# Three edits to a four-layer block: how expert weights are split, how combination weights are made, and in which order side steps run

## The chip, the cores and the metric

One core of a Trainium2 chip runs the whole program. The metric is the device time of one execution in microseconds; three runs of the kernel before gave a median of 966.74 us. A profile was taken of one more execution.

## What is computed

Four rows of 1024 tokens by 128 features pass through four residual layers: a linear attention of its own kind, a mixture of experts (MoE), a windowed softmax attention, and the same MoE again. Only the MoE is touched by the arithmetic of the change:

```python
logits = x @ gate_w.T
probs = jax.nn.softmax(logits.astype(jnp.float32), axis=-1)
top_w, top_idx = jax.lax.top_k(probs, TOP_K)          # 8 of 32 experts
top_w = top_w / jnp.sum(top_w, axis=-1, keepdims=True)
...
gu = x @ guw.T
g, u = jnp.split(gu, 2, axis=-1)
y = u * jax.nn.silu(g) @ dw.T                         # weighted by comb, summed over experts
```

## The kernel before

**Stages.** A row is cut into two halves of 512 tokens (four tiles of 128). Every half passes twice through the MoE, which makes 16 MoE stages of 16 chunks; a chunk is two experts. For a chunk TensorE forms gate and up (`gate_up`, lines 1519 to 1521: six products), ScalarE applies silu (L1056), VectorE multiplies by up (L1304), GpSimd multiplies by the combination weights spread over the partitions (L872), and TensorE adds the down product to one bank (L1542). Work tiles form a ring of 6. The windowed attention is a stretch of its own in each row: eight tiles, each with scores, maxima (VectorE), exponentials (ScalarE, L1081), a normalisation (GpSimd, L880), transpositions and their copies (VectorE, L1346) and the mix. The order is the list `SCHEDULE`: period 0 has the stages "first" and "third" and then "attn" of row 0; later periods interleave two rows.

**Side steps.** Everything else (norms, q/k/v, linear attention, router, combination weights, projections) is cut into named steps. The table `PLAN` says behind which chunk of a stage, or behind which of three hooks of an attention tile (slot 0 to 26), a step stands; every engine runs its own part of a step at that place of its own queue, in order. `own`, `ahead` and `back` choose the row: this period's, the next, the one before. The list `AHEAD` is the order of all that comes before the first chunk; this stretch is called the opening here. Steps that go through PSUM share one bank, `side`, in the order of the plan.

Steps that the prediction speaks of: `x_stats` (VectorE norm statistics, waits for the load of the row's half), `attend` (GpSimd key-value terms), `kvsum`, `wterm`, `wred` (VectorE, linear attention), `qkv`/`qkv_next` (TensorE and ScalarE), `h_...` (head norms), `moe_turn`, `z_hi`, `z_lo` (the MoE's input, transposed and split), `route`, `r_sum`, `top` (router logits and their eight largest), `weigh` (ScalarE: exponentials), `comb` (VectorE: keep the chosen, sum, reciprocal), `cnorm` (ScalarE), `weighT` (transposed by TensorE, copied to `combT`, L1025). SyncE then sends `combT` to DRAM (L649) and spreads it back in four quarters, the first as eight DMAs (L661), the others as two (L666). It issues in one order: the weights of the next stage, then the loads of the next row's x (L631), then the last quarters.

**Split weights.** Gate and up weights are loaded once into `spread_w`, before that buffer is used for combination weights, and kept as a rounded high half and a low remainder. VectorE makes both high halves (`w_hi`, L1170) and the low half of up (`w_lo` 1, L1176); GpSimd makes the low half of gate in four pieces (`w_lo` 0, L768).

**Combination weights.** `top` finds the largest logits, negates the first (L1276) and marks the chosen (L1278); `weigh` waits for the negated maximum only:

```python
for t in range(T):
    a = act.activation(expd[:, t], logits[:, t], ACT.Exp, bias=neg_top[:, t:t + 1])
```

## Time and profile before

| | us |
|---|---|
| runs | 966.5, 979.81, 966.74 |
| median | 966.74 |
| profiled execution | 970.32 |
| its span, first to last instruction | 968.5 |

The page gives the share of the span in which each engine was busy, then groups of instructions by line and shape. "Chain" is the chain of work that ended last, followed back from the end: what stands in it had nothing else covering it. A window row gives each engine's busy time in a stretch. PE is TensorE, PEld its weight loads, DVE is VectorE, ACT is ScalarE, POOL is GpSimd, SP is SyncE; PEclk is TensorE's granted clock as a share of 2.4 GHz.

### The profile page before, as it was taken

What the parts mean: (1) busy time and instruction counts of PE and PEld (TensorE: products, weight loads), DVE (VectorE), ACT (ScalarE), POOL (GpSimd) and SP (SyncE); (2) the same over time, 40 slices, a digit from 0 to 9 for tenths busy, and PEclk for the clock granted to TensorE, in tenths of its full rate; (3) what the DMA queues carried; (4) which work ended last, traced back from release to release, by engine and by line L of the source; (5) the groups of instructions that cost most, each with busy time, mean ns of one, the idle gap of its engine ahead of it and who ended that gap; (6) DMA issues with size and microseconds to landing.
All of it is one profiled execution on the core that took longest, in us unless ns stands there. A gap on an engine that the chain in (4) does not pass through costs nothing.

```text
span 968.5 us, 16816 instructions
## 1 busy us (share of the span) xinstructions
PE 895.2 (92%) x5456; PEld 623.2 (64%) x5456; DVE 653.0 (67%) x1471; ACT 611.6 (63%) x1876; POOL 663.8 (69%) x617
## 2 busy tenths in 40 slices
PE   2467999898999999999999999999999999999998
PEld 1145666685667666687666666687666667667665
DVE  5898876897768748698648756798635348447522
ACT  4446676993665576795775585896556377486531
POOL 6786888675687759576669768666666545646654
PEclk8559999999899999999999999999999999999999
DMA  6006254016343626240433534340344530713352
GB/s 193 0 1 142 52 128 89 2 46 136 64 123 76 139 60 157 58 121 13 98 92 87 146 83 108 74 129 17 87 106 102 135 68 27 159 38 102 88 133 65
DMA packets 64903, 85.75 MB, mean 89 GB/s; under 512 B 5232, under 2 KB 30768, under 8 KB 64560
## 3 DMA queue, kind: packets, MB, share of 16 engines
q1 hardware_dynamic: 64816, 84.68, 36.4%
q8 instruction: 43, 0.70, 0.3%
q14 instruction: 44, 0.36, 0.1%
HBM read 79.39 MB, written 5.28 MB: 87 GB/s over the span
## 4 chain that ended last, share of the span: by engine, by line
PE 69%; DVE 10%; ACT 7%; POOL 5%; issue 4%; DMA 3%; SPq 1%; DVEq 0%; ACTq 0%; POOLq 0%
PE bank L1542 19%; PE bank L1519 11%; PE bank L1521 10%; PE bank L1520 10%; ACT probs L1081 4%; PE bank L1578 4%; PE bank L1563 3%; PE bank L1592 2%; POOL work L872 2%; DVE probsT L1346 2%; PE bank L1406 1%; DMA spread_w<-comb_dram 1%; DVE w_terms L1188 1%; PE bank L1556 1%; DMA x_buf<-x 1%
## 5 line engine op out<-in xcount | busy, mean ns | idle before, releaser
L872 POOL TENSOR_TENSOR work<-work,spread_w 128x512 f32<-128x512 f32 x256 | 333.8, 1318 | 171.0 <-DVE work L1304 151.7
L1304 DVE TENSOR_TENSOR work<-work,bank 128x512 f32<-128x512 f32 x256 | 172.1, 683 | 185.3 <-PE bank L1521 93.1
L1542 PE MATMUL bank<-work,down_w 128*128 128x512 f32 x512 | 262.7, 598 | 1.9 <-POOL work L872 1.9
L1056 ACT ACTIVATE work<-bank 128x512 f32<-128x512 f32 x256 | 150.3, 596 | 176.5 <-PE bank L1521 171.9
L1519 PE MATMUL bank<-z_hi,gate_hi 128*128 128x512 f32 x256 | 168.0, 656 | 4.9 <-ACT work L1056 2.7
L1081 ACT ACTIVATE probs<-bank,neg_max 128x96 f32<-128x96 f32 x512 | 166.3, 386 | 5.5 <-DVE neg_max L1332 3.9
L880 POOL TENSOR_TENSOR probs<-probs,prob_inv 128x768 f32<-128x768 f32 x64 | 95.1, 1486 | 59.9 <-DVE prob_inv L1340 59.6
L1081 ACT ACTIVATION_READ_ACCUMULATOR probs<-bank,neg_max 128x1 f32 x512 | 127.6, 252 | 0.0
L1542 PEld LDWEIGHTS bank<-work,down_w 128*128 128x128 f32 x512 | 95.3, 189 | 29.6 <-POOL work L872 5.6
L1519 PE MATMUL bank<-z_hi,up_hi 128*128 128x512 f32 x256 | 101.8, 397 | 3.1 <-DVE work L1304 3.1
L1521 PE MATMUL bank<-z_hi,gate_lo 128*128 128x512 f32 x256 | 102.0, 398 | 0.0
L1521 PE MATMUL bank<-z_hi,up_lo 128*128 128x512 f32 x256 | 101.5, 397 | 0.0
L1520 PE MATMUL bank<-z_lo,gate_hi 128*128 128x512 f32 x256 | 101.2, 395 | 0.0
L1520 PE MATMUL bank<-z_lo,up_hi 128*128 128x512 f32 x256 | 100.4, 392 | 0.0
L829 POOL TENSOR_TENSOR kv_terms<-elu,qkv 128x1024 f32<-128x1024 f32 x32 | 81.8, 2562 | 12.5 <-DVE elu L1153 7.2
L1346 DVE COPY probsT<-bank 96x512 f32<-96x512 f32 x128 | 80.2, 666 | 3.6 <-PE bank L1578 3.2
L1332 DVE TENSOR_REDUCE neg_max<-bank 128x4 f32<-128x384 f32 x128 | 64.8, 547 | 20.1 <-PE bank L1563 19.2
L1519 PEld LDWEIGHTS bank<-z_hi,gate_hi 128*128 128x128 f32 x256 | 49.0, 191 | 42.4 <-issue 31.0
L1578 PE MATMUL bank<-ident,probs 128*96 128x128 f32 x512 | 69.8, 278 | 6.8 <-DVE probsT L1346 6.0
L1520 PEld LDWEIGHTS bank<-z_lo,gate_hi 128*128 128x128 f32 x256 | 49.3, 193 | 33.7 <-issue 30.6
L1563 PE MATMUL bank<-keysT,qm 32*128 32x96 f32 x1024 | 69.2, 269 | 0.0
L1563 PEld LDWEIGHTS bank<-keysT,qm 32*128 32x128 f32 x1024 | 66.4, 188 | 0.0
(155 smaller groups left out, 1467.2 us busy)
## 6 DMA issues: line engine op xcount, KB each, us to landing
spread_w<-comb_dram SPq DMA_DIRECT2D x96, 512.0 KB, 6.7
spread_w<-comb_dram SPq DMA_DIRECT2D x128, 128.0 KB, 3.0
vals<-v_dram SPq DMA_DIRECT2D x16, 384.0 KB, 4.0
x_buf<-x SPq DMA_DIRECT2D x8, 256.0 KB, 4.3
v_dram<-v_tok SPq DMA_DIRECT2D x8, 256.0 KB, 6.8
out<-xs SPq DMA_DIRECT2D x8, 256.0 KB, 3.1
spread_w<-wg SPq DMA_DIRECT2D x1, 1024.0 KB, 7.1
spread_w<-wu SPq DMA_DIRECT2D x1, 1024.0 KB, 9.2
```

Source lines behind the costliest of these rows:

```text
L872: pool.tensor_tensor(work[:, n % WORK], work[:, n % WORK], spread_w[:, n // EACH % 2, s % EACH], ALU.mult).then_inc(hid_gated, 1)
L880: pool.tensor_tensor(pr, pr, prob_inv[:, i % 2, part].unsqueeze(2).broadcast_to([P, HALF_BLOCKS, KW]), ALU.mult).then_inc(probs_normed, 1)
L1056: act.activation(work[:, n % WORK], bank[GATE_BANKS[ring_of(row, f, s)]], ACT.Silu).then_inc(silu_ready, 1)
L1081: a = act.activation(probs[:, i % 2, m], bank[hg][:, b * KW:(b + 1) * KW], ACT.Exp, bias=neg_max[:, i % 2, m:m + 1], accum_out=prob_sum[:, ...
L1304: dve.tensor_tensor(work[:, n % WORK], work[:, n % WORK], bank[UP_BANKS[ring_of(row, f, s)]], ALU.mult).then_inc(gated_ready, 1)
L1346: dve.tensor_copy(probsT[:, b], bank[4 + b % 2][0:KW, :]).then_inc(probsT_copied, 1)
L1519: pe.matmul(dst, w_hi[:, cols], h, start=True, stop=False)
L1520: pe.matmul(dst, w_hi[:, cols], l, start=False, stop=False)
L1521: pe.matmul(dst, w_lo[:, cols], h, start=False, stop=True).then_inc(ready, 1)
L1542: pe.matmul(bank[Y_BANK], down_w[:, c], work[:, n % WORK], start=(c == 0), stop=(c == CH - 1)).then_inc(down_done, 1)
L1563: mm = pe.matmul(bank[hg][:, KW * b:KW * (b + 1)], qm[feats, i // T, NB * (i % T) + b].rearrange("p j q -> p (j q)"), keysT[feats, first:f ...
L1578: mm = pe.transpose(bank[4 + b % 2][0:KW, P * hg:P * (hg + 1)], probs[:, i % 2, hg * NB + b], ident[:])
```

## The change

High halves are made by ScalarE, as two copies of 128x2048. Low halves are made in eight pieces of 128x512 (`w_lo` 0 to 7): TensorE multiplies the full weights by the identity, adds the high half times the negated identity in the same PSUM bank, and ScalarE copies the bank out. GpSimd makes the negated identity at the start. `top` now subtracts the maximum and one more from the logits, after the chosen are marked; `weigh` is one silu of 128x128, and `comb` recovers exp(z) as silu(z) / (z - silu(z)): a subtraction, a reciprocal and a product more. The plan and the opening have a new order throughout; the places that the text speaks of are shown.

```diff
     (0, "first"): {
-        2: own(("h_pow2", 1), ("h_newton2", 1), ("h_scale", 1)),
-        4: own(("h_gain", 1), ("h_sum", 1)) + ahead(("wterm", 0), ("wred", 0), ("kvsum", 1)) + own(("x_add", 1)),
...
-        14: ahead(("wred", 2)) + own(("weighT", 1)) + ahead(("kvsum", 3), ("wterm", 3)),
...
+        3: ahead(("qscale", 0), ("attend", 1)) + own(("x_add", 1)),
+        5: ahead(("kvsum", 0)) + own(("attnT", 1)) + ahead(("wterm", 0)),
...
+        15: own(("weighT", 1)) + ahead(("wred", 3), ("h_sq1", 0), ("h_red1", 0), ("h_newton1", 0), ("h_g2", 0)),
     },
...
     (0, "attn"): {
-        0: ahead(("wred", 4), ("wterm", 5), ("z_hi", 0)),
+        0: ahead(("kvsum", 5), ("wred", 4), ("moe_turn", 0), ("z_hi", 0)),
         1: ahead(("z_lo", 0)),
-        2: own(("y_back", 1), ("s_stats", 1), ("s_rstd", 1)),
-        4: ahead(("wred", 5)) + own(("s_apply", 1)),
-        5: own(("seq_copy", 1)),
+        3: own(("y_back", 1), ("s_stats", 1), ("s_rstd", 1)),
+        4: own(("s_apply", 1)),
+        5: ahead(("wterm", 5), ("wred", 5)) + own(("seq_copy", 1)),
         6: own(("seq_turn", 1), ("keys_copy", 1)),
         7: own(("keys", 1)),
-        8: own(("queries", 1)) + ahead(("attend", 7)) + own(("queries_copy", 1)),
-        10: ahead(("route", 0), ("r_sum", 0)),
-        11: own(("values", 1)) + ahead(("top", 0), ("weigh", 0)),
-        13: own(("bias", 1)),
-        15: ahead(("comb", 0), ("cnorm", 0)),
-        22: own(("proj", 0)),
+        8: own(("queries", 1)) + ahead(("kvsum", 6)) + own(("queries_copy", 1)),
+        9: ahead(("wterm", 6)),
+        10: own(("bias", 1)),
+        11: ahead(("route", 0), ("r_sum", 0), ("top", 0), ("weigh", 0)),
+        13: ahead(("comb", 0)) + own(("values", 1)),
+        19: ahead(("cnorm", 0)),
+        20: ahead(("attend", 7)) + own(("proj", 0)),
+        22: ahead(("weighT", 0)),
         23: own(("m_stats", 2), ("m_rstd", 2)),
-        25: ahead(("weighT", 0)),
     },
...
     (1, "first"): {
-        0: back(("m_apply", 2)) + own(("kvsum", 6), ("wterm", 6)),
-        2: back(("proj", 1)) + own(("wred", 6), ("kvsum", 7)),
-        3: own(("wterm", 7)) + back(("moe_turn", 2)) + own(("wred", 7)) + ahead(("x_stats", 0)),
...
+        0: back(("m_apply", 2)),
+        2: own(("wred", 6)),
+        3: back(("proj", 1)) + ahead(("x_stats", 0), ("x_rstd", 0)),
+        4: own(("kvsum", 7), ("wterm", 7)) + back(("moe_turn", 2)),
...
     },
...
 AHEAD = (
-    own(("masks", 0), ("x_stats", 0), ("x_rstd", 0), ("x_apply", 0), ("x_turn", 0), ("lam", 0),
-        ("qkv_first", 0), ("qkv_first", 1), ("qkv_first", 2), ("elu_first", 0), ("masks", 1), ("attend", 0),
-        ("x_stats", 1), ("elu_first", 1), ("qkv_first", 3), ("w_hi", 0), ("kvsum", 0), ("elu_first", 2),
-        ("elu_first", 3), ("wterm", 0), ("attend", 1), ("x_rstd", 1), ("wred", 0), ("kvsum", 1), ("wterm", 1),
-        ("attend", 2), ("kvsum", 2), ("attend", 3), ("wred", 1), ("x_apply", 1), ("wterm", 2), ("x_turn", 1),
-        ("w_lo", 0), ("qkv", 4), ("kvsum", 3), ("wred", 2), ("wterm", 3)) + ahead(("x_stats", 0)) + own(("qkv", 5),
-        ("wred", 3), ("w_hi", 1), ("h_sq1", 0), ("h_red1", 0), ("h_g2", 0), ("h_sq2", 0)) + ahead(("x_rstd", 0)) +
-        own(("h_newton1", 0), ("h_red2", 0), ("h_pow2", 0), ("h_newton2", 0), ("h_scale", 0), ("qkv", 6),
-        ("qkv", 7), ("expo", 1), ("h_gain", 0), ("elu", 1), ("h_sum", 0), ("attend", 4), ("qscale", 1),
-        ("attnT", 0), ("x_add", 0), ("kvsum", 4), ("wterm", 4), ("mlp1", 0), ("mlp2", 0), ("m_stats", 0),
-        ("attend", 5), ("attend", 6)) + ahead(("x_apply", 0), ("x_turn", 0)) + own(("m_rstd", 0)) +
-        ahead(("qkv_next", 0)) + own(("wred", 4), ("kvsum", 5), ("wterm", 5), ("wred", 5), ("kvsum", 6),
-        ("m_apply", 0), ("moe_turn", 0), ("w_lo", 1), ("z_hi", 0), ("z_lo", 0), ("wterm", 6), ("wred", 6)) +
-        ahead(("qkv_next", 1)) + own(("route", 0), ("r_sum", 0), ("attend", 7), ("early", 0), ("top", 0),
-        ("weigh", 0)) + ahead(("qkv_next", 2)) + own(("kvsum", 7), ("comb", 0), ("wterm", 7), ("masks", 2),
-        ("wred", 7), ("cnorm", 0), ("h_sq1", 1)) + ahead(("qkv_next", 3)) + own(("h_red1", 1), ("h_newton1", 1)) +
-        ahead(("expo", 0), ("elu", 0)) + own(("early", 1), ("early", 2), ("weighT", 0), ("lead", 0), ("lead", 1),
-        ("h_g2", 1)) + ahead(("attend", 0)) + own(("h_sq2", 1), ("early", 3), ("early", 4), ("early", 5)) +
-        ahead(("qscale", 0)) + own(("h_red2", 1), ("lead", 2)) + ahead(("attend", 1), ("kvsum", 0)) +
-        own(("lead", 3), ("lead", 4), ("lead", 5))
+    own(("masks", 0), ("x_stats", 0), ("x_rstd", 0), ("x_apply", 0), ("x_stats", 1), ("lam", 0), ("x_turn", 0),
+        ("qkv_first", 0), ("masks", 1), ("x_rstd", 1), ("qkv_first", 1), ("qkv_first", 2), ("elu_first", 0),
+        ("qkv_first", 3), ("elu_first", 1), ("attend", 0), ("attend", 1), ("elu_first", 2), ("x_apply", 1),
+        ("w_hi", 0), ("kvsum", 0), ("wterm", 0), ("wred", 0), ("attend", 2), ("kvsum", 1), ("elu_first", 3),
+        ("x_turn", 1), ("w_lo", 0), ("qkv", 4), ("wterm", 1), ("w_hi", 1), ("kvsum", 2), ("wred", 1), ("attend", 3),
+        ("wterm", 2), ("qkv", 5), ("w_lo", 1), ("kvsum", 3), ("wred", 2), ("wterm", 3), ("wred", 3), ("h_sq1", 0),
+        ("h_g2", 0)) + ahead(("x_stats", 0)) + own(("h_red1", 0)) + ahead(("x_rstd", 0)) + own(("h_newton1", 0),
+        ("h_sq2", 0), ("h_red2", 0), ("h_pow2", 0), ("h_newton2", 0), ("h_scale", 0), ("qkv", 6), ("qkv", 7),
+        ("expo", 1), ("elu", 1), ("h_gain", 0), ("h_sum", 0), ("attend", 4), ("qscale", 1), ("attnT", 0),
+        ("x_add", 0), ("attend", 5), ("kvsum", 4), ("wterm", 4), ("mlp1", 0), ("mlp2", 0), ("m_stats", 0),
+        ("attend", 6)) + ahead(("x_apply", 0)) + own(("m_rstd", 0)) + ahead(("x_turn", 0)) + own(("m_apply", 0),
+        ("w_lo", 2), ("w_lo", 3), ("wred", 4), ("kvsum", 5), ("wterm", 5), ("moe_turn", 0), ("wred", 5),
+        ("z_hi", 0), ("kvsum", 6), ("w_lo", 4), ("w_lo", 5), ("z_lo", 0), ("route", 0), ("attend", 7), ("wterm", 6),
+        ("r_sum", 0), ("wred", 6)) + ahead(("qkv_next", 0)) + own(("w_lo", 6), ("top", 0)) + ahead(("qkv_next", 1),
+        ("qkv_next", 2)) + own(("kvsum", 7), ("wterm", 7), ("wred", 7), ("weigh", 0), ("comb", 0), ("w_lo", 7),
+        ("masks", 2)) + ahead(("qkv_next", 3)) + own(("h_sq1", 1), ("h_g2", 1), ("h_red1", 1), ("h_newton1", 1)) +
+        ahead(("expo", 0), ("elu", 0)) + own(("early", 0), ("early", 1)) + ahead(("attend", 0)) + own(("cnorm", 0),
+        ("early", 2), ("weighT", 0), ("h_sq2", 1), ("h_red2", 1), ("h_pow2", 1), ("lead", 0), ("h_newton2", 1),
+        ("early", 3), ("h_scale", 1), ("lead", 1), ("lead", 2), ("lead", 3), ("h_gain", 1), ("h_sum", 1),
+        ("lead", 4), ("early", 4), ("early", 5), ("lead", 5))
 )
...
+        minus_ident = sb("minus_ident", [P, P], F32R)
...
         hi_ready, router_ready = sem("hi_ready"), sem("router_ready")
-        gate_lo_ready, up_lo_ready = sem("gate_lo_ready"), sem("up_lo_ready")
+        minus_ready, split_ready, lo_ready = sem("minus_ready"), sem("split_ready"), sem("lo_ready")
...
                 if k < 2:
-                    sp.wait_ge(*((gate_lo_ready, EACH), (up_lo_ready, 1))[k])
+                    sp.wait_ge(lo_ready, EACH * (k + 1))
...
                                pattern=[[-1, P]], channel_multiplier=1).then_inc(ident_ready, 1)
+            pool.wait_ge(ident_ready, 1)
+            pool.tensor_scalar(minus_ident[:], ident[:], -1.0, None, ALU.mult).then_inc(minus_ready, 1)
...
             const(pool.memset(minus_half[:], -0.5))
-
-            def w_lo(row, n):
-                if n == 0:
-                    pool.wait_ge(gate_loaded, 16)
-                    pool.wait_ge(hi_ready, 1)
-                    for part in range(EACH):
-                        pool.wait_ge(w_terms_ready, T - 1 + part // 2)
-                        cols = slice(GT * part, GT * (part + 1))
-                        pool.tensor_tensor(gate_lo[:, cols], spread_w[:, 0, part], gate_hi[:, cols],
-                                           ALU.subtract).then_inc(gate_lo_ready, 1)
...
         def _(act):
+            def w_hi(row, n):
+                act.wait_ge((gate_loaded, up_loaded)[n], 16)
+                act.activation((gate_hi, up_hi)[n][:], spread_w[:, n].rearrange("p c t -> p (c t)"),
+                               ACT.Copy).then_inc(hi_ready, 1)
+
+            def w_lo(row, k):
+                act.wait_ge(split_ready, k + 1)
+                cols = slice(GT * (k % EACH), GT * (k % EACH + 1))
+                act.activation((gate_lo, up_lo)[k // EACH][:, cols], bank[k % T], ACT.Copy).then_inc(lo_ready, 1)
+
...
                 act.wait_ge(top_ready, STAGE_AT[row, f] + 1)
-                for t in range(T):
-                    a = act.activation(expd[:, t], logits[:, t], ACT.Exp, bias=neg_top[:, t:t + 1])
-                a.then_inc(expd_ready, 1)
+                act.activation(expd[:], logits[:], ACT.Silu).then_inc(expd_ready, 1)
...
-            def w_hi(row, n):
-                dve.wait_ge((gate_loaded, up_loaded)[n], 16)
-                dve.tensor_copy((gate_hi, up_hi)[n][:],
-                                spread_w[:, n].rearrange("p c t -> p (c t)")).then_inc(hi_ready, 1)
-
-            def w_lo(row, n):
-                if n == 1:
-                    dve.wait_ge(hi_ready, 2)
-                    dve.tensor_tensor(up_lo[:], spread_w[:, 1].rearrange("p c t -> p (c t)"), up_hi[:],
-                                      ALU.subtract).then_inc(up_lo_ready, 1)
-
...
                 step(ins)
-                dve.tensor_scalar(neg_top[:], top[:, :, 0], -1.0, None, ALU.mult).then_inc(top_ready, 1)
+                dve.tensor_scalar(neg_top[:], top[:, :, 0], -1.0, -1.0, ALU.mult, ALU.add)
...
                 step(ins)
+                dve.tensor_tensor(logits[:], logits[:], neg_top[:].unsqueeze(2).broadcast_to([P, T, NE]),
+                                  ALU.add).then_inc(top_ready, 1)
...
                     dve.wait_ge(side_ready, SIDE_AT[STREAM[fg - 1][0], "weighT", STREAM[fg - 1][1]] + 1)
+                step(dve.tensor_tensor(logits[:], logits[:], expd[:], ALU.subtract))
+                step(dve.reciprocal(logits[:], logits[:]))
...
                                               op0=ALU.is_lt, op1=ALU.mult))
+                step(dve.tensor_tensor(comb[:], comb[:], logits[:], ALU.mult))
...
+            def w_lo(row, k):
+                n, part = k // EACH, k % EACH
+                if k == 0:
+                    pe.wait_ge(minus_ready, 1)
+                if part == 0:
+                    pe.wait_ge(hi_ready, n + 1)
+                if k < T:
+                    pe.wait_ge(relu_ready, k + 1)
+                else:
+                    pe.wait_ge(lo_ready, k - T + 1)
+                pe.matmul(bank[k % T], ident[:], spread_w[:, n, part], start=True, stop=False)
+                pe.matmul(bank[k % T], minus_ident[:], (gate_hi, up_hi)[n][:, GT * part:GT * (part + 1)],
+                          start=False, stop=True).then_inc(split_ready, 1)
+
...
                 if n == 0:
-                    pe.wait_ge(gate_lo_ready, EACH)
-                    pe.wait_ge(up_lo_ready, 1)
+                    pe.wait_ge(lo_ready, 2 * EACH)
...
```

## Rows read from the trace of the kernel before

**Rows 1.** The page, busy time and share of each engine.
```profile
PE 895.2 (92%) x5456; PEld 623.2 (64%) x5456; DVE 653.0 (67%) x1471; ACT 611.6 (63%) x1876; POOL 663.8 (69%) x617
```

**Rows 2.** Busy time by stretch: start:end, length; per engine busy (x instructions); PEclk, DMA share, GB/s.
```profile
40.00:60.00 20.00, 10.26 (x27) 5.36 (x27) 16.87 (x29) 11.07 (x23) 15.87 (x13) 0.50 0.00 1
60.00:84.00 24.00, 17.08 (x54) 11.94 (x54) 21.04 (x43) 13.42 (x29) 17.02 (x16) 0.73 0.12 39
...
172.00:229.00 57.00, 53.81 (x682) 43.15 (x679) 49.59 (x121) 47.82 (x247) 37.49 (x42) 0.97 0.10 30
230.00:280.00 50.00, 46.40 (x169) 30.97 (x169) 34.07 (x70) 29.96 (x57) 32.93 (x29) 0.93 0.50 114
...
406.00:456.00 50.00, 47.66 (x654) 38.67 (x654) 43.48 (x92) 41.36 (x232) 33.68 (x34) 1.00 0.28 72
...
500.00:539.00 39.00, 39.00 (x154) 26.52 (x153) 31.54 (x65) 20.71 (x42) 34.59 (x28) 1.00 0.33 79
```

**Rows 3.** Chain that ended last, first 100 us: start, length, what.
```profile
17.09 1.14 DVE gate_hi L1170
...
35.86 1.35 DVE up_hi L1170
...
60.51 0.40 DVE up_lo L1176
60.91 1.72 issue
...
71.24 1.23 DVE attn L1194
...
75.95 0.60 ACT combT L1025
```

**Rows 4.** The same chain, 98 to 172 us.
```profile
111.08 1.28 ACT L1056
```

**Rows 5.** The same chain, 172 to 290 us.
```profile
215.39 0.89 PE bank L1495 x8
...
222.55 0.59 ACT combT L1025
...
231.54 8.77 DMA x_buf<-x
...
251.65 0.23 PE bank L1521
...
252.58 0.86 PE bank L1542 x2
```

**Rows 6.** Waits: total us, times, longest us.
```profile
DVE stats L1139 <- DMA x_buf<-x: 8.3, 2, 4.5
```

**Rows 7.** Groups by shape: xcount | busy us, mean ns | idle before, releaser.
```profile
L1188 DVE TENSOR_TENSOR w_terms<-elu,kv 128x1024 f32<-128x1024 f32 x32 | 44.8, 1400 | 1.7 <-DVE x_buf L1246 0.2 <-DVE logits L1266 0.2
L1056 ACT ACT_TABLE_LOAD x32 | 41.1, 1283 | 1.3 <-ACT combT L1025 0.6 <-ACT v_tok L1048 0.2
...
L1164 DVE TENSOR_REDUCE kv<-kv_terms 128x64 f32<-128x1024 f32 x32 | 38.9, 1214 | 7.9 <-POOL kv_terms L829 7.6
...
L1012 ACT ACT_TABLE_LOAD x15 | 19.2, 1283 | 0.3
...
L1007 ACT ACTIVATE z_hi<-bank 128x512 fp32r<-128x512 f32 x16 | 9.6, 603 | 10.5 <-PE bank L1400 10.5
...
L972 ACT ACTIVATE elu<-elu 128x1024 f32<-128x1024 f32 x7 | 7.4, 1060 | 0.1
...
L1286 DVE SCALAR_TENSOR_TENSOR comb<-replaced,expd 128x128 f32<-128x128 f32 x16 | 6.7, 416 | 7.9 <-ACT expd L1012 7.3 <-DVE replaced L1278 0.4
...
L1266 DVE TENSOR_TENSOR logits<-logits,bank 128x128 f32<-128x128 f32 x16 | 4.6, 288 | 0.6
...
L1232 DVE RECIPROCAL newton<-head_ms 128x64 f32<-128x64 f32 x8 | 4.4, 553 | 0.3
...
L1170 DVE CAST up_hi<-spread_w 128x2048 fp32r<-128x2048 f32 x1 | 1.4, 1435 | 0.0
```

More of the change, by code:

```diff
@@ new lines @@
+        6: own(("mlp1", 1), ("mlp2", 1), ("m_stats", 1), ("m_rstd", 1)),
+        7: ahead(("attend", 2), ("x_stats", 1), ("x_rstd", 1)),
+        8: ahead(("wred", 0), ("kvsum", 1)) + own(("m_apply", 1)),
+        9: ahead(("attend", 3)),
+        10: own(("moe_turn", 1), ("z_hi", 1)) + ahead(("wterm", 1), ("wred", 1)),
+        11: own(("z_lo", 1)) + ahead(("kvsum", 2)) + own(("route", 1), ("r_sum", 1), ("top", 1)) +
+            ahead(("x_apply", 1), ("x_turn", 1)),
+        12: own(("weigh", 1)) + ahead(("qkv", 4)) + own(("comb", 1)),
@@ L188 @@
[L188 to L196 removed]
+        1: ahead(("mlp2", 0)),
@@ new lines @@
+        2: ahead(("m_stats", 0), ("m_rstd", 0)),
+        4: own(("y_back", 1), ("s_stats", 1), ("s_rstd", 1)),
+        5: own(("queries", 0)) + ahead(("wterm", 4)),
+        6: ahead(("attend", 6)),
+        7: ahead(("wred", 4), ("kvsum", 5), ("m_apply", 0)) + own(("s_apply", 1)),
+        8: ahead(("moe_turn", 0), ("z_hi", 0), ("z_lo", 0), ("wterm", 5)),
+        9: ahead(("route", 0), ("r_sum", 0), ("top", 0), ("weigh", 0), ("comb", 0)),
+        10: own(("seq_turn", 1)),
+        11: own(("keys", 1)) + ahead(("cnorm", 0), ("attend", 7), ("wred", 5), ("kvsum", 6)),
@@ L232 @@
-        7: own(("y_back", 0)),
-        8: ahead(("attend", 3), ("kvsum", 1)),
-        10: own(("weigh", 1), ("s_stats", 0), ("comb", 1)),
-        11: ahead(("wterm", 1), ("wred", 1), ("kvsum", 2)) + own(("cnorm", 1), ("s_rstd", 0)),
-        13: ahead(("wterm", 2), ("wred", 2)) + own(("s_apply", 0)),
-        14: ahead(("kvsum", 3), ("wterm", 3), ("wred", 3)),
-        15: own(("weighT", 1)),
+        0: own(("moe_turn", 1), ("z_hi", 1), ("z_lo", 1)),
+        2: own(("route", 1), ("r_sum", 1), ("top", 1)),
@@ L249 @@
[L249 to L254 removed]
+        0: back(("m_apply", 3)) + ahead(("kvsum", 2), ("qkv", 4)),
+        1: ahead(("wterm", 2), ("qkv", 5), ("wred", 2)),
@@ new lines @@
+        2: ahead(("kvsum", 3), ("wterm", 3)),
+        3: ahead(("qkv", 6)),
+        4: ahead(("qkv", 7), ("wred", 3), ("h_sq1", 0), ("h_red1", 0), ("h_newton1", 0)),
+        5: back(("moe_turn", 3), ("z_hi", 3), ("z_lo", 3)),
+        7: back(("route", 3)) + ahead(("expo", 1)) + back(("r_sum", 3), ("top", 3)) + ahead(("elu", 1),
+            ("attend", 4)) + back(("weigh", 3)),
+        8: back(("y_back", 2)) + ahead(("qscale", 1)),
+        9: back(("comb", 3), ("cnorm", 3)) + ahead(("h_g2", 0), ("h_sq2", 0)),
```

350 lines of the change are left out of this document (164 added, 186 removed).

## The prediction

> **What bounds the kernel now.** I read the page first, then a table of stretches, then the chain in order of time, then the waits, and last the groups by shape for prices. The page has TensorE busy for 92% of the span and the three other engines between 63% and 69% [rows 1]. That average hides two kinds of stretch, and the table of stretches parts them [rows 2]. A middle MoE stage (500 to 539) has TensorE busy for 39.00 of 39.00 us, with DVE at 31.54, ACT at 20.71 and POOL at 34.59: whatever the change takes off ACT or puts on DVE there is covered, as long as DVE keeps some of its 7.5 us of room. The opening is different: from 40 to 60 PE has 10.26 of 20 and a clock of 0.50, DVE 16.87. Here the chain runs through DVE [rows 3]. The third kind is an attention stretch: row 0's (172 to 229) has DVE at 49.59 and ACT at 47.82 of 57, row 1's (406 to 456), with fewer side steps, 43.48 and 41.36 of 50. All engines are nearly full there, and each can be the one that comes last. One more place stands out: the stage from 230 to 280 takes 50 us with PE at 46.40 and a mean clock of 0.93. In the chain the combination weights are copied at 222.55, SyncE then issues spreads, and only at 231.54 a load of x, which takes 8.77 us [rows 5]; DVE stood up to 4.5 us before `x_stats` for such a load [rows 6], and later products wait behind it.
>
> So there are four places where time can be had or lost: the opening, the first stage, attention of row 0, and the stage behind it. From 280 on PE is full, or the stretch is an attention that the change hardly reloads.
>
> **Part 1, the weight halves, in the opening.** DVE loses two casts and one subtraction of 128x2048. On the chain they are 1.14, 1.35 and 0.40 us, and the piece of 1.72 us behind the last is put down to nothing: there DVE was still in that subtraction [rows 3]. The subtraction thus costs the path between 0.40 and 2.12; I take 1.8, near the upper end, because nothing else on DVE can start under it. That is 1.14 + 1.35 + 1.8 = 4.3 us off the path. POOL loses its four pieces, which were on no part of the chain, so I count nothing for them.
>
> What is added lies on ACT and PE. The cast of 128x2048 on ACT: 512 columns take 603 ns and 1024 take 1060 [rows 7], 0.89 ns a column, so 1060 + 1024 x 0.89 = 1.97 us, twice; eight copies of 0.60 make 4.8. ACT has room in the opening, but two of the pieces stand before `z_hi` and two more between it and `weigh`. On PE a piece is a full-precision pair of 0.86 us and one rounded product of 0.23 at full clock [rows 5], 1.09 us; at half clock, which is what the stretch from 40 to 60 was granted [rows 2], 2.18. Pieces 4 and 5 stand between `moe_turn` and `route`, so up to 4.4 us of products before the router, against two conversions (0.60 and as much again) that `route` must await anyway. DVE covers the rest with one `wterm` (1.40) before it needs `r_sum`. The price is 0 to 3 us; I take 1.5, as the denser products may bring the full clock earlier. The negated identity is one small POOL operation ahead of work that then waits for DVE: nothing, and at most half a microsecond if that cover is gone.
>
> The Trainium skill ("ScalarE: Activation LUTs", *Rules for kernel authors*) says to give simple element-wise work to VectorE and not to ScalarE. The casts agree with it: 1.435 us on DVE [rows 7] against 1.97 estimated on ACT. By that rule the two casts would cost 2 x 0.54 = 1.1 us instead of giving anything; but the engine on the chain here is DVE, so I keep the sum above.
>
> **Part 2, silu for exp.** Each of 16 stages gets on DVE an addition of 128x128, a subtraction and a product (0.29 each by the nearest form), and a reciprocal of 128x128: half the width takes 553 ns, so between 0.55 and 1.11; I take 1.0 [rows 7]. That is 1.9 us a stage. `weigh` now also waits for the marking. On ACT four small exponentials become one silu, and a table load before it and one behind it go: there are 15 and 32 such loads of 1283 ns at these two lines [rows 7]. Fourteen stages lose both; in the opening and in row 0's attention silu stands among exponentials, and three loads are added. 28 - 3 = 25 loads, 32 us of ACT. On the chain I find only one of them, at 111.08 [rows 4]. In the PE-full stages both changes are hidden.
>
> In the opening, `comb` also moves behind the last `wterm` and `wred`. The old path from the end of that last sum, 71.24 + 1.23 = 72.5, to the copy at 75.95 went through ACT and PE and took 3.5 us [rows 3]. The new one needs `comb` (its 0.42 and a reduction as now, and 1.6 new: some 2.3), while ACT does copies and a square of some 1280 columns (1.5 at 603 ns for 512) and the exponential with its load (1.28 + 1.06), 3.8 in all; then come `cnorm` and the transpositions, about 1.5: 5.3. So +1.8, less 0.7 because `comb` no longer stands before that sum, and +0.3 for `top`. Opening: -4.3 + 1.5 + 1.8 - 0.7 + 0.3 = -1.4, and I add -0.6 for statistics moved into a place where DVE idles: **-2**, range -7 to +3.
>
> **Part 3, the new order.** First stage: the head-norm steps of half 1 are done in the opening while the spread is under way, and the load of 1.28 goes [rows 4]: **-2**, range -4 to +1. SyncE's issues keep their order; the waits for low halves ahead of the first two quarters are over by then.
>
> Attention of row 0 receives on DVE `kvsum` 5 and 6 (1.21 each), `wterm` 6 (1.40) and 1.9 for Part 2: 5.7 us; and on ACT two table loads less the saved exponentials, 1.9. If DVE and ACT share the limit, half of the 7.6 shows: **+4**, from 0 to 11 (all of it, with one more fall of the clock). POOL's `attend` 7 stands late, before the last tile's normalisation; I leave that inside the range.
>
> The stage behind it: `weighT` goes from slot 25 to 22. The step that stood at slot 22, `proj` 0, ran at 215.39 and the copy of slot 25 at 222.55 [rows 5], so the send and everything that SyncE has behind it, the x load too, start up to 6.7 us earlier, while `x_stats` stays in slot 3. The wait of 4.5 us goes [rows 6]; and the mean clock of 0.93 over 50 us is 7 us at half speed, which costs 3.5 [rows 2]. Of 8 I take **-6**, range -8 to 0. What is late next is the spread of the weights itself, not x.
>
> From 280 on: **0**, range -3 to +5. Later attention stretches lose or gain single steps, and `weighT` in the second half of row 3's attention goes from slot 5 to 10 of 15, which its DMA chain still allows.
>
> **Sum.** -2 - 2 + 4 - 6 + 0 = -6. The profiled execution took 970.32 us, so 964.3; it lies 3.6 above the median of the runs. From the median the sum gives 966.74 - 6 = 961.
>
> **The rivals.** (A) *Slower: row 0's attention takes all that is put on it.* All 7.6 us are on the path and a gap lets the clock fall once more (3.5): +11, so 966.74 - 2 - 2 + 11 - 6 = 968. For it: DVE was at 87% there and ACT at 84%. Against: the table already shows that stretch longer than row 1's partly by its projections, which are PE work. It decides from +10 on.
>
> (B) *No change: the x load is not what holds the stage.* It is late because the spreads before it fill the queue, and if these, earlier or not, hold the first chunks, the 6 us stay: 967. For it: SyncE issues in one order and spreads stand first. Against: DVE's wait names x.
>
> (C) *The loads of tables were on the path after all.* A load holds ACT before every silu that follows, so 25 x 1.283 = 32 us go: 935. Against: ACT is at 53% in the middle stage, and one load in the chain is all I find.
>
> The Trainium skill ("ScalarE: Activation LUTs", *What ACT_TABLE_LOAD costs*) gives 2.66 us for every switch of the set, of which 1.283 is the load and the rest a drain. The rows have the 1283 ns exactly, but only 1.3 us of idle before 32 of them, so no drain shows; by its figure 25 switches would be 66 us.
>
> (D) *The opening and the first stage come to their lower ends*, and attention costs nothing: -7 - 4 + 0 - 8 = -19, so 948. For it: DVE really is the chain there. Against: `route` stands behind the identity products.
>
> **How the numbers follow.** The forecast, 961 with 955 to 967 of its own, has 0.54; A 0.15, B 0.15, C 0.07, D 0.09. Leaving out C, half of D and the upper third of A, 0.16 in all, gives 948 to 971. Two per cent, about what a measurement of this kernel can tell from no change, is 19 us: below 947.4 lie C and about half of D, 0.11; above 986 only an A with a further stall, 0.03; within, 0.86.
>
> **What would show it.** In the changed kernel's chain the copy of `combT` in the opening near 74 us instead of 75.95, with no DVE line for the halves; a first stage without a table load; row 0's attention longer by about 4 us, DVE above 90% of it; no wait of `x_stats` for x beyond the first, and no half clock in the stage behind; table loads at `weigh` down from 15 to 2 and at the chunks' silu from 32 to about 18; stages from 280 on of the same length. I am wrong if `r_sum` waits several microseconds for `route`, if that attention grows by 10, or if the stage behind it still takes 50 us.

## The result, and the profile after

The changed kernel takes 982.25 us (median of 4 runs, 979.21 to 984.54), the kernel before 966.91 beside it. The ratio is 1.0133, with an interval of 1.0103 to 1.0163: 1.3% slower, 13 us, where 961 was forecast. The profiled execution took 984.54 us with a span of 982.8, so its stretches can be held against those of the profiled execution before (span 968.5). The ratios here leave out executions more than 1.5% above the fastest of their kernel, among the experiments below the profiled ones of e2 (with three more of its ten), e5 and e13.

The page of the changed kernel, to be held against [rows 1]:

```profile
PE 911.0 (93%) x5480; PEld 634.4 (65%) x5480; DVE 687.2 (70%) x1532; ACT 577.2 (59%) x1813; POOL 658.2 (67%) x614
```

DVE has 34 us more, ACT 34 less, as the parts of the change said. TensorE has 16 us more, and these totals don't say where. The 24 identity products alone take 19.2 us:

```profile
L1424 PE MATMUL bank<-spread_w,ident 128*128 128x512 f32 x16 | 11.0, 776 | 0.7 <-issue 0.7
...
L1425 PE MATMUL bank<-gate_hi,minus_ident 128*128 128x512 f32 x4 | 5.0, 1261 | 0.0
...
L1425 PE MATMUL bank<-up_hi,minus_ident 128*128 128x512 f32 x4 | 3.2, 796 | 0.0
```

But they all lie in the opening, where TensorE's busy time grew by 5.7 us only. Row 0's and row 1's attention have 6.8 and 5.7 us more of it in the tables below, with about as many products (683 for 692, 659 for 654): there products take longer. That points to the clock.

To find the place, I cut both traces at the same work: at the first or last down projection of a stage. First the kernel before, by the table of stretches (columns as in [rows 2]): opening, first stage, row 0's attention, the stage behind it, row 1's attention.

```profile
0.00:84.40 84.40, 40.04 (x102) 23.33 (x103) 66.27 (x128) 40.56 (x92) 61.36 (x67) 0.68 0.21 68
84.40:128.00 43.60, 40.20 (x154) 25.67 (x153) 35.99 (x80) 26.02 (x53) 32.95 (x31) 1.00 0.52 116
170.40:230.20 59.80, 55.77 (x692) 44.40 (x691) 51.69 (x125) 49.97 (x254) 39.99 (x44) 0.97 0.11 32
230.20:278.40 48.20, 44.65 (x158) 29.50 (x159) 32.59 (x68) 29.12 (x55) 31.13 (x26) 0.93 0.48 110
406.10:457.00 50.90, 48.15 (x654) 38.74 (x652) 44.32 (x96) 41.92 (x232) 34.58 (x35) 1.00 0.28 71
```

The same five stretches of the changed kernel, and behind them four short pieces of row 0's attention:

```profile
0.00:83.30 83.30, 45.71 (x126) 25.50 (x127) 66.96 (x136) 49.80 (x102) 54.25 (x65) 0.77 0.23 74
83.30:125.30 42.00, 39.55 (x154) 25.89 (x153) 36.63 (x77) 22.12 (x46) 33.89 (x29) 1.00 0.42 94
...
169.20:239.40 70.20, 62.59 (x683) 49.29 (x681) 55.69 (x131) 52.32 (x253) 40.30 (x43) 0.83 0.16 41
239.40:282.00 42.60, 42.34 (x166) 28.19 (x167) 32.53 (x73) 25.46 (x49) 30.26 (x26) 1.00 0.43 105
410.10:466.90 56.80, 53.86 (x659) 44.29 (x658) 47.02 (x101) 42.30 (x233) 34.85 (x35) 0.88 0.27 65
...
177.00:179.00 2.00, 0.54 (x20) 0.27 (x12) 1.97 (x2) 0.85 (x3) 2.00 (x2) 0.93 0.01 4
181.00:183.00 2.00, 2.00 (x12) 1.57 (x12) 1.18 (x3) 2.00 (x12) 1.47 (x1) 0.50 0.04 8
203.00:205.00 2.00, 0.82 (x11) 0.57 (x11) 1.97 (x4) 2.00 (x15) 0.00 (x0) 1.00 0.00 0
211.00:213.00 2.00, 2.00 (x17) 1.79 (x16) 1.20 (x3) 0.00 (x0) 0.00 (x0) 0.50 1.19 247
```

Read the lengths first: -1.1, -1.6, **+10.4**, -5.6, **+5.9**. Then the clock, the third number from the end (1.00 is 2.4 GHz). A mean of 0.83 over 70.2 us means 2 x 0.17 x 70.2 = 23.9 us at half clock (1.2 GHz instead of 2.4), and work at half clock takes twice as long, so up to 11.9 us are lost (all of it if TensorE has work throughout); before, 0.97 over 59.8 us gives 1.8. The difference, 10.1, is nearly the growth of the attention; by busy time 6.8 of the 10.4 are longer products and 3.6 more idle time of TensorE. The short pieces show what went ahead of each fall: TensorE busy for 0.54 and for 0.82 of 2 us, and a little later the clock at 0.50 while TensorE is busy without a break. DVE's share of this attention did not rise above 90%, as I had put down as a sign; it fell from 86% to 79%. A stretch that grows while its supposed limit idles more is held by something else.

The waits of TensorE in that attention name the first gap: `seq_turn` waits for the `z` of row 0's second half.

```profile
PE bank L1398 <- ACT z L937: 2.3, 1, 2.3
```

Row 1's attention has another cause. These are SyncE's waits in it, first in the kernel before, then in the changed one, with TensorE's own wait behind them (SPq is SyncE's queue; L649, or L653 after, sends the weights, L682 loads the windows of values):

```profile
SPq L649 <- ACT combT L1025: 17.3, 1, 17.3
SPq L682 <- PE bank L1592: 9.0, 1, 9.0
```

```profile
SPq L653 <- ACT combT L1029: 25.5, 1, 25.5
...
PE bank L1603 <- DMA vals<-v_dram: 1.3, 1, 1.3
```

SyncE issues in order, and the send of the weights, which waits for `combT`, stands ahead of the send of the values. Before, the values were ready 9.0 us early (SyncE had to wait that long for the old windows to be free). With `weighT` in slot 5 SyncE waits 8.2 us longer for `combT`, and now TensorE waits for the values. The chain of the changed kernel shows it link by link (start, length, what):

```profile
418.42 0.32 ACT combT L1029
418.76 1.80 DMA comb_dram<-combT
420.58 0.47 SPq L665
...
426.87 7.88 DMA v_dram<-v_tok
...
435.21 5.35 DMA vals<-v_dram
440.60 1.10 PE bank L1603 x32
```

The wait itself is 1.3 us; behind it the clock falls here too, 2 x 0.12 x 56.8 = 13.6 us at half speed, and the attention grows by 5.9.

The second stage is 1.5 us longer, and the other stretches from 282 us on add +4.8, no more than 3.2 in one of them (the first stage of row 2 +2.2, the last stage +1.8). The groups of table loads and of the new operations on DVE came as forecast:

```profile
L1060 ACT ACT_TABLE_LOAD x17 | 21.8, 1283 | 0.7 <-ACT combT L1029 0.5
...
L1017 ACT ACT_TABLE_LOAD x3 | 3.8, 1283 | 0.1
...
L1282 DVE RECIPROCAL logits<-logits 128x128 f32<-128x128 f32 x16 | 15.2, 953 | 0.6
...
L1285 DVE TENSOR_TENSOR comb<-comb,logits 128x128 f32<-128x128 f32 x16 | 7.6, 478 | 0.5
...
L1273 DVE TENSOR_TENSOR logits<-logits,neg_top 128x128 f32<-128x128 f32 x16 | 7.0, 435 | 0.5
L1281 DVE TENSOR_TENSOR logits<-logits,expd 128x128 f32<-128x128 f32 x16 | 6.4, 397 | 3.2 <-ACT expd L1017 3.2
```

### The profile page after: what moved, and what is told of

The parts are those of the page before. It is cut to its first block, busy times and chain, and to the rows that moved or that the text cites. A ratio compares the mean times of both kernels' runs of the same rounds, so it can differ in the third digit from the quotient of the medians.

```text
span 982.8 us, 16859 instructions
## 1 busy us (share of the span) xinstructions
PE 911.0 (93%) x5480; PEld 634.4 (65%) x5480; DVE 687.2 (70%) x1532; ACT 577.2 (59%) x1813; POOL 658.2 (67%) x614
## 4 chain that ended last, share of the span: by engine, by line
PE 50%; DVE 6%; ACT 6%; POOL 4%; issue 3%; DMA 3%; SPq 1%; DVEq 0%; ACTq 0%; POOLq 0%
PE bank L1553 16%; PE bank L1530 8%; PE bank L1532 8%; PE bank L1531 8%; ACT probs L1085 4%; PE bank L1589 2%; PE bank L1574 2%; POOL work L868 1%; DVE probsT L1344 1%; DMA vals<-v_dram 1%; PE bank L1603 1%; POOL probs L876 1%; DVE work L1302 1%; SPq L665 1%; PE bank L1404 1%
## 5 line engine op out<-in xcount | busy, mean ns | idle before, releaser
L1085 ACT ACTIVATION_READ_ACCUMULATOR probs<-bank,neg_max 128x1 f32 x512 | 122.7, 240 | 0.0
L1589 PE MATMUL bank<-ident,probs 128*96 128x128 f32 x512 | 77.0, 298 | 7.8 <-DVE probsT L1344 6.1
L1589 PEld LDWEIGHTS bank<-ident,probs 128*96 128x96 f32 x512 | 58.9, 136 | 21.6 <-issue 12.4
L1574 PE MATMUL bank<-keysT,qm 32*128 32x96 f32 x1024 | 72.4, 279 | 0.0
```

The costliest lines, as they stand in the source:

```text
L1085: a = act.activation(probs[:, i % 2, m], bank[hg][:, b * KW:(b + 1) * KW], ACT.Exp, bias=neg_max[:, i % 2, m:m + 1], accum_out=prob_sum[:, ...
L1574: mm = pe.matmul(bank[hg][:, KW * b:KW * (b + 1)], qm[feats, i // T, NB * (i % T) + b].rearrange("p j q -> p (j q)"), keysT[feats, first:f ...
L1589: mm = pe.transpose(bank[4 + b % 2][0:KW, P * hg:P * (hg + 1)], probs[:, i % 2, hg * NB + b], ident[:])
```

## The experiments

A profile is one execution, and these differ by several us with the clock, so each verdict takes the profile for the place and the ratio to the kernel before for the size. The profiled executions of e2, e3, e5 and e13 are long ones of their kernels (989.87, 994.76, 988.79 and 989.72 us against medians of 982.07, 987.41, 980.54 and 984.58), and that of e6 is the shortest of its ten (971.6 against 977.22), so the length of one attention below is no size by itself.

**e1: SyncE's order in row 1's attention.** In the changed kernel's plan for `(1, "attn")`:

```diff
-        5: ahead(("weighT", 0)),
+        0: ahead(("weighT", 0)),
```

> The changed kernel, in row 1's attention weighT back in slot 0. My theory: SyncE issues in order, so the send of the weights (which waits for combT) stands ahead of the send of the values, and combT in slot 5 makes the values late; then row 1's attention falls from 56.8 us to about 51, its half clock goes, and the time is 977 (5 us below the 982 of the changed kernel, between 4 and 7). Rival: that attention is longer because of the work put on DVE by the silu form; then the time stays within 1 us of 982 and the attention at 56 or more.

Ratio 1.0108 (1.0052 to 1.0164). Row 1's attention, and SyncE's wait for the old windows in it:

```profile
416.10:467.30 51.20, 48.00 (x656) 39.17 (x656) 46.27 (x101) 41.82 (x232) 35.07 (x35) 1.00 0.26 73
```

```profile
SPq L686 <- PE bank L1603: 8.8, 1, 8.8
```

The 8.8 us of slack are back, and the attention is 5.6 us shorter with no half clock. The place is shown, and other traces bear it out: with `weighT` in slot 5, row 1's attention fell to half clock in three of five (56.8, 57.8 and 56.9 us in the changed kernel, e2 and e13, against 52.0 and 52.1 in e5 and e12), with slot 0 in none of five of this family (51.2 or 51.3; e1, e8, e10, e14, e15). The total did not move clear of noise. In the profiled execution, the longest of four, the stage behind row 0's attention took 48.5 us instead of 42.6 and the opening 85.5 instead of 83.3; whether the other three gained the 5.6 us is not known.

**e2 and e3: is row 0's attention longer by the order or by the silu form?** e2 gives the changed kernel the old places of that attention's steps; e3 gives the kernel before the silu form.

```diff
 e2, (0, "attn"):
-        0: ahead(("kvsum", 5), ("wred", 4), ("moe_turn", 0), ("z_hi", 0)),
+        0: ahead(("wred", 4), ("wterm", 5), ("z_hi", 0)),
...
+        15: ahead(("comb", 0), ("cnorm", 0)),
+        22: own(("proj", 0)) + ahead(("weighT", 0)),
 e3, weigh:
-                    a = act.activation(expd[:, t], logits[:, t], ACT.Exp, bias=neg_top[:, t:t + 1])
+                act.activation(expd[:], logits[:], ACT.Silu).then_inc(expd_ready, 1)
...
```

> The changed kernel, with the side steps of row 0's attention in the places they had before (kvsum 6 and wterm 6 back behind it, kvsum 5 and moe_turn ahead of it), weighT left in slot 22. Theory order: most of the 10.5 us come from the places of the steps, so that attention falls from 70.3 us to about 63 and the time to 976 (7 us below the changed kernel, between 4 and 9). Rival arithmetic: they come from what the silu form puts on DVE and ScalarE there; the attention stays at 67 or more and the time at 979 or above.

> The kernel before, in its own order, with silu in place of exp and nothing else. Theory order: row 0's attention grows by 2 to 4 us, the other stretches by under 1 each, the time is 969 (967 to 971), DVE busy rises by 34 us and the table loads at weigh fall from 15 to 2. Rival arithmetic: row 0's attention alone grows by 8 or more, with a second half-clock stretch, and the time is 975 or above. Third: the 25 or so table loads saved give time: below 964.

e2 has ratio 1.0069 (1.0026 to 1.0112), e3 1.0176 (1.0114 to 1.0238). Row 0's attention in e2, then in e3:

```profile
169.40:244.90 75.50, 68.23 (x683) 55.15 (x683) 54.57 (x129) 52.54 (x253) 40.84 (x44) 0.77 0.16 42
```

```profile
174.40:250.20 75.80, 69.40 (x691) 56.20 (x691) 56.08 (x130) 52.56 (x253) 39.88 (x44) 0.77 0.09 26
```

By the traces my theory fell: the silu form alone, in the old order, makes that attention as long as the whole change does, and costs 1.8%, no less than the change. In e3 ACT got 2.6 us more work in that attention and DVE 4.4; it grew by 16.0, of which up to (0.23 x 75.8) - 1.8 = 15.6 us is lost to the clock: 691 products for 692 took 13.6 us longer. Both are long executions, though. By the ratio e2 is some 6 us below the changed kernel (1.0069 against 1.0133), inside the 4 to 9 that the theory had forecast, so the order has a price as well.

**e4: the two moves of weighT alone**, in the kernel before.

```diff
-        22: own(("proj", 0)),
+        22: own(("proj", 0)) + ahead(("weighT", 0)),
-        25: ahead(("weighT", 0)),
...
-        0: ahead(("weighT", 0)),
-        5: back(("y_back", 3)),
+        5: ahead(("weighT", 0)) + back(("y_back", 3)),
```

> The kernel before with weighT moved as in the change, in row 0's attention from slot 25 to 22 and in row 1's from 0 to 5, nothing else. Theory: the stage behind row 0's attention is shorter by 5 to 6 us, row 1's attention longer by 5 to 6 with a wait of TensorE for the values of 2 us or more, the time within 1.5 us of 967. Rivals: the second move costs nothing in the old order (then 961), or the first gives nothing by itself (then 972).

Ratio 0.9988 (0.9957 to 1.0019). Row 0's attention, the stage behind it, row 1's attention, and TensorE's longest wait in the last:

```profile
169.40:232.20 62.80, 57.10 (x691) 45.97 (x691) 51.95 (x125) 49.97 (x254) 41.07 (x44) 0.95 0.19 52
232.20:273.00 40.80, 40.80 (x159) 27.44 (x158) 30.09 (x68) 29.25 (x56) 31.10 (x26) 1.00 0.41 98
400.30:455.70 55.40, 50.08 (x658) 40.40 (x656) 44.64 (x96) 42.03 (x233) 34.49 (x35) 0.97 0.23 66
```

```profile
PE bank L1466 <- ACTq L1025: 2.9, 1, 2.9
```

Gain and loss are where I expected them: the stage behind is 7.4 shorter, row 1's attention 4.5 longer. (The attention ahead is 3.0 longer, but e10 and e15, with `weighT` in the same slot, have 59.9 there.) But the second has another mechanism than in the changed kernel. Here `y_back` stands in the same slot behind `weighT` and waits 2.9 us for the side bank, since ACT makes `combT` only after its exponentials; the values were not waited for.

**e5 to e8: the silu form taken apart.** e5 is the changed kernel with the exponential form for the one stage whose weights are made in row 0's attention. e6 and e7 add to the kernel before, at that stage alone, only the table loads or only the DVE operations. e8 is the changed kernel with the exponential form everywhere and e1's edit.

```diff
 e5
+                if STAGE_AT[row, f] == 2:
+                    for t in range(T):
+                        a = act.activation(expd[:, t], logits[:, t], ACT.Exp, bias=neg_top[:, t:t + 1])
...
 e6
+                if STAGE_AT[row, f] == 2:
+                    act.activation(tiny[:], neg_top[:, 0:1], ACT.Silu)
 e7
+                if fg == 2:
+                    step(dve.tensor_tensor(spare[:], logits[:], expd[:], ALU.subtract))
+                    step(dve.reciprocal(spare[:], spare[:]))
...
```

> The changed kernel, with the exponential form of the combination weights kept for one of the 16 stages, the one whose weights are made inside row 0's attention. Theory table loads: the silu there puts a load of its table and a load of the exponentials' table in the middle of that attention's exponentials, ScalarE is late with probs, TensorE gets gaps and its clock falls; without it that attention goes from 70 us to about 62 and its second half-clock stretch is gone, ratio to before about 1.004. Rival, the new order: the attention stays at 67 or more, ratio 1.010 or more.

> The kernel before, with one silu of 128x1 into a tile that nobody reads put ahead of the exponentials of weigh in row 0's attention: two more table loads on ScalarE there, nothing on VectorE. Theory table loads: that attention goes from 59.8 us to 65 or more, with 10 us or more of added half clock behind slot 11; time 972 to 980 where before has 967 to 971. Rival, VectorE's four operations: it grows by 0 to 3 us.

> The kernel before, with the silu form's four VectorE operations (addition, subtraction, reciprocal, product of 128x128) done into a tile that nobody reads, for the weights made in row 0's attention alone; ScalarE unchanged. Theory table loads: that attention grows by 0 to 3 us and the time by as much. Rival, VectorE: it grows by 5 us or more, with a half-clock stretch behind slot 13.

> The changed kernel with the exponential form of before in all stages and weighT of row 1's attention back in slot 0: new weight halves and new order alone. Theory (the loss is the silu form in attention and that one step): opening and first stage 3 us shorter, row 0's attention at 60 to 63, the stage behind it 5 to 6 shorter, row 1's attention at 51, ratio 0.990 to 0.996. Rival, the new order itself costs: row 0's attention at 66 or more, ratio 1.000 or above.

Ratios: e5 1.0093 (1.0066 to 1.0121), e6 1.0056 (1.0025 to 1.0087), e7 1.0043 (1.0011 to 1.0075), e8 1.0116 (1.0060 to 1.0171). Row 0's attention in the four, in this order:

```profile
171.10:241.40 70.30, 64.48 (x682) 51.66 (x682) 54.46 (x126) 50.42 (x254) 40.33 (x43) 0.81 0.14 38
```

```profile
169.70:233.00 63.30, 56.56 (x690) 45.29 (x691) 51.45 (x125) 52.79 (x257) 40.09 (x44) 0.95 0.10 31
```

```profile
170.30:232.90 62.60, 57.07 (x691) 45.29 (x691) 53.28 (x129) 49.96 (x254) 40.03 (x44) 0.95 0.11 31
```

```profile
167.10:234.70 67.60, 61.55 (x682) 49.71 (x680) 54.35 (x126) 50.53 (x254) 40.35 (x43) 0.85 0.16 40
```

By their ratios neither half of the silu form is free: e6, with 2.8 us more on ACT, costs 5.4 us, and e7, with 1.6 more on DVE, 4.2. In their traces that attention is 3.5 and 2.8 longer than before, but both lengths lie inside what kernels with neither half show (58.4 to 63.7, table below); neither half alone brings the long half-clock stretch of e3. Whether both together cost more than their sum is open: by the ratios e3 costs some 9 us more than e11 below, which keeps the exponentials there and in the opening, and e6 and e7 add up to 9.6. e5 and e8 say that the new order tips the clock without any silu there. So the theory "table loads" is too small by itself (63.3 us where 65 or more was expected), and its rival "order" holds. e8 shows one more thing, in the first stage of row 2 (49.8 us against 42.7): the order was fitted to the silu form. With exponentials, ACT has four table loads in 10 us where `weigh`, a chunk's silu and the Gelu of `mlp1` follow each other, and TensorE waits for that Gelu's result:

```profile
PE bank L1401 <- ACT attnT L1009: 3.8, 1, 3.8
```

**e9 to e12: putting together what holds.** e9 keeps the new weight halves, opening and first two stages, and from row 0's attention on has the old order (with `weighT` in slot 22) and the exponentials. e10 is the changed kernel with three things undone: e1's edit, e2's and e5's. e11 is the kernel before with silu in all stages but the opening's and that of row 0's attention. e12 is e5 with this edit:

```diff
-        3: own(("y_back", 1), ("s_stats", 1), ("s_rstd", 1)),
+        2: own(("y_back", 1), ("s_stats", 1), ("s_rstd", 1)),
-        5: ahead(("wterm", 5), ("wred", 5)) + own(("seq_copy", 1)),
...
```

> The new weight halves with the new opening and first two stages, then the order of before from row 0's attention on (weighT there in slot 22), exponentials everywhere. Theory: opening and first stages 2 to 4 us shorter, attention and the stage behind it together 1 to 5 shorter, the rest as before; ratio 0.990 to 0.997, faster than both kernels. Rival: any change ahead of it lets row 0's attention fall to the half clock again, 66 us or more, ratio 1.003 or above.

> The changed kernel with three things undone together: the exponential form for the weights made in row 0's attention, the old places of that attention's steps, weighT of row 1's attention in slot 0. Theory (each alone tips the clock, together they are the loss in the two attentions): row 0's attention at 60 to 64 us with under 8 of half clock, row 1's at 51 with none, ratio 0.998 to 1.004. Rival (something else, such as the new stages ahead of it, tips the clock): row 0's attention at 67 or more, ratio 1.007 or above.

> The kernel before in its own order with the silu form in 14 of 16 stages: not in the one made in the opening and not in the one made in row 0's attention. Theory: the 16 us that the silu form costs alone arise in these two places; left are some 4 us in the stages; ratio 1.000 to 1.006, row 0's attention at 60 to 63. Rival: the silu form loads VectorE everywhere and makes every attention late; ratio 1.010 or more.

> The changed kernel with the exponential form in row 0's attention (as in the run before) and there wterm 5, wred 5, y_back 1 and its norm back in slots 0, 4 and 2. Theory: the half-clock stretch of 10 us near 180 us is gone or 3.4 us at most, as TensorE no longer waits for seq_turn's z; the attention falls by 3 us or more against the run without that move. Rival: the stretch near 180 stays, it comes from the full load and not from that wait.

**e9 is faster than both kernels**: 964.24 us against 968.98 beside it, ratio 0.9934 (0.9904 to 0.9965). Its opening, row 0's attention and the stage behind it:

```profile
0.00:80.90 80.90, 47.48 (x127) 26.23 (x128) 64.44 (x132) 49.11 (x105) 54.66 (x65) 0.77 0.23 76
...
167.20:230.90 63.70, 58.22 (x692) 47.33 (x692) 51.98 (x125) 50.11 (x254) 41.06 (x44) 0.92 0.19 51
230.90:271.60 40.70, 40.70 (x159) 27.33 (x158) 30.07 (x68) 29.14 (x56) 30.98 (x26) 1.00 0.43 97
```

The opening is 3.5 us shorter, attention and next stage together 3.6. e10 has ratio 1.0056 (1.0034 to 1.0078), above the 1.004 that I had allowed, though row 0's and row 1's attention are as before, row 0's without any half clock:

```profile
170.40:230.30 59.90, 53.32 (x683) 42.27 (x683) 51.34 (x125) 49.77 (x254) 40.83 (x44) 1.00 0.18 51
400.60:451.80 51.20, 47.88 (x654) 39.09 (x655) 46.40 (x101) 41.67 (x232) 34.86 (x35) 1.00 0.29 72
...
623.40:680.10 56.70, 54.21 (x659) 44.61 (x658) 45.30 (x100) 41.86 (x232) 36.25 (x36) 0.88 0.25 63
```

What it still loses in this trace lies from 280 us on, half of it in row 2's attention (last line), which takes 51.2 us at full clock in the kernel before.

e11 has ratio 1.0084 (1.0058 to 1.0110) and row 0's attention at 58.4 us, clock 1.00: the 16 us of e3 do arise with the silu there. But what is left is more than I allowed: the opening grew by 1.6 and the rest by 6.3 in sum (no stage by more than 2.1), though 28 table loads were gone. e12 has ratio 1.0127 (1.0072 to 1.0182), and that attention at 73.0 us with a clock of 0.74: my reason for the first fall, `y_back` one slot late, was wrong. Moved forward it meets another wait:

```profile
PE bank L1493 <- DVE z_lo L1256: 1.3, 1, 1.3
```

`moe_turn`, now in slot 0, holds the side bank until DVE has made `z_lo`, and `y_back` comes behind it.

**e13 to e15: head or tail of the order, and row 2.** What was open by then: which part of the new order tips row 0's attention, and whether `weighT` in slot 3 instead of 0 is the price in row 2's. Head means `kvsum` 5 and `moe_turn` in slot 0, tail the new places from slot 8 on. e13 is e12 with the head's two steps back ahead of the attention; e14 is e10 with just these two in slot 0; e15 is e10 with `weighT` of row 2's attention in slot 0.

> As the run with wterm and y_back in their old slots, and kvsum 5 and moe_turn 0 back in the third stage, ahead of row 0's attention. Theory head: moe_turn in slot 0 keeps the side bank until z_lo, so y_back (and all that hangs on it) comes late and TensorE waits; without it no half clock before 195 us, the attention at 62 to 67. Rival tail: kvsum 6, wterm 6, comb and values in their new slots decide; a half-clock stretch of 10 us or more behind 195 stays and the attention is at 67 or more.

> The changed kernel with the three things undone, and kvsum 5 and moe_turn 0 at the head of row 0's attention again as in the change. Theory head: the half-clock stretch within the first 20 us of that attention is back, 6.8 us or more of it, the attention goes from 59.9 us to 63 or more. Rival tail: it stays below 62 with at most 3.4 us of half clock.

> The changed kernel with the three things undone, and weighT of row 2's attention in slot 0 instead of 3. Theory SyncE: the values are there in time, TensorE's wait for them (1.1 us) and the half clock of 13.7 us near 660 go, row 2's attention falls from 56.7 us to 51 or 52, and the ratio from 1.0056 to about 1.001. Rival: that half clock comes from something else, the attention stays at 55 or more.

Ratios: e13 1.0123 (1.0053 to 1.0192), e14 1.0064 (1.0028 to 1.0099), e15 1.0079 (1.0033 to 1.0125). Row 0's attention in e13, then in e14, then row 2's in e15:

```profile
168.70:236.40 67.70, 63.59 (x683) 51.32 (x682) 53.15 (x125) 50.38 (x254) 39.83 (x44) 0.82 0.15 40
```

```profile
169.60:235.40 65.80, 59.88 (x683) 48.83 (x683) 52.40 (x127) 50.30 (x254) 41.56 (x44) 0.87 0.17 48
```

```profile
621.80:687.90 66.10, 62.66 (x654) 51.66 (x653) 46.62 (x100) 42.17 (x232) 36.33 (x36) 0.74 0.22 54
```

In these traces head and tail each suffice: with the head out the clock still falls, with the head alone in (and the same 1.3 us wait for `z_lo` as in e12) it falls too. In time the head alone costs nothing clear of noise (1.0064 against e10's 1.0056). e15 refutes my theory for row 2: with the values in time that attention ran at half clock for 34 us. In e10 and e14, whose code for it is the same and has `weighT` in slot 3, it took 56.7 and 51.9. What tips it was not found.

Row 0's attention in us, in the traces with all of its steps in the old or the new places (`weighT` in slot 25 or 22 among the old):

| | exponential form | silu form |
|---|---|---|
| old places of the steps | 59.8 (before), 62.8 (e4), 63.7 (e9), 59.9 (e10, e15), 58.4 (e11) | 75.8 (e3), 75.5 (e2) |
| new places | 70.3 (e5), 67.6 (e8) | 70.2 (changed kernel), 67.6 (e1) |

The two don't add up; either one lets the clock fall. What makes a gap tip the clock in one execution and not in another stays open.

## Why the prediction was wrong, by its own steps

- **Opening, -2: not borne out.** The profile has -1.1, and the first `combT` is copied at 72.6 us where near 74 was forecast. But over all traces this opening takes 83.3 to 85.5 us (nine, mean 84.2) and the old one 83.5 to 84.4 (four, mean 84.0): no gain clear of this spread. The halves and the new order do gain, some 2.7 (81.7 and 80.9 in e8 and e9, which have no silu there); the silu form takes as much back, where my net of the terms behind `comb` was +1.4. The four new operations on DVE are 0.4 of that: 0.95 + 0.48 + 0.44 + 0.40 = 2.3 us, not 1.9.
- **First stage, -2: right** (-1.6; 41.9 to 42.2 us in the traces with the whole new order and the silu form, 43.4 to 43.6 before). The sum had no term for the second stage, which is 1.5 longer.
- **Stage behind row 0's attention, -6: right** (-5.6, no half clock; `x_stats` still waits 2.0 us for x), and the cause was the move of `weighT`, as e4 shows. It is not safe: in e1 and e13, with `weighT` in the same slot, `x_stats` waited 5.5 and 6.0 us and the stage took 48.5 and 49.1 at a clock of 0.93.
- **Table loads: the counts right** (3 and 17 for 2 and 18), and they were not on the path: rival (C) is out, as e11 has most of the loads saved and is slower. The Trainium skill ("ScalarE: Activation LUTs", *What ACT_TABLE_LOAD costs*) puts a drain beside each load; e6's two loads added 2.8 us of busy time on ACT, 2 x 1.283 and the small silu, and no row shows a drain.
- **"Attention of row 0 ... half of the 7.6 shows: +4": the step that failed**, by size. It was +10.4. I priced added work as a share of that work and let the clock fall once more for 3.5 us at most. The work was below what I had added up (4.0 us on DVE and 2.4 on ACT, for 5.7 and 1.9); what grew was the half clock, from 3.6 to 23.9 us, up to 10.1 of the 10.4. The silu form (e2, e3) or the new places (e5, e8) bring such stretches each by itself; with neither, that attention takes 58.4 to 63.7. Rival (A) came near with +11, but out of 7.6 us of work and 3.5 of clock: that is luck. I had the row that warned of it: DVE at 87% and ACT at 84% of that stretch with the clock at 0.97 [rows 2] is a place where it already falls at times.
- **"From 280 us on: 0": the other step that failed.** It was +10.7. I checked `weighT` of row 3's attention against its DMA chain and did not do so for row 1's, moved from slot 0 to 5, where SyncE has the values queued behind the weights: +5.9, shown by e1 (and not in every execution: 52.0 and 52.1 us in e5 and e12). The rest, +4.8, was not taken apart between the new order and the silu form; "in the PE-full stages both changes are hidden" did not hold either (e11, silu in 14 stages of the old order: 8 us by its ratio).

Rival (A)'s sum, 968, lies inside the range of 948 to 971; the second step carried the time out of it.

## What to carry to other kernels

Where TensorE's work is short products and two helpers are nearly full (here 87% and 84%), price an added step by what a gap does to the clock, not by its own length. A mean clock under 1.00 in such a stretch is a warning, but 1.00 is no all-clear: the attentions of rows 1 and 2 had it before the change. For a step whose result is sent by a queue that issues in order, list what stands behind the send and how many us of slack it has (here 9.0, and 8 were used) before moving it. Undo suspected parts together as well as one by one: in the traces either one undone left row 0's attention about as long as it was (e2, e8), both undone gave it back whole (e10, e15). And hold every trace against the times of its kernel: e2's is of a long execution, and by the ratio e2 took back half of the loss.
